# An AdaLN and grouped-expert FFN kernel: expert tiles in another order, rounded terms first, and one weight store and one load of scales moved

## What is computed

```
h      = einsum('bct,bcd->bdt', x, weights[conditions])        # 4096 tokens x 256
scores = sigmoid(h @ gate_w.T)
sb     = scores + gate_bias
# group score: sum of the 2 largest of 8; the 2 best of 4 groups; in them the 8 largest sb
wsel   = scores[chosen 8]; wsel = wsel / wsel.sum() * 2.5       # cw: zero elsewhere
x_lat  = h @ fc1_w.T                                            # 128 wide
y_lat  = sum over experts e of cw[:, e] * relu2(x_lat @ w1[e].T) @ w2[e].T
shared = relu2(h @ shared_up_w.T) @ shared_down_w.T             # 512 wide inside
out    = x + shared + y_lat @ fc2_w.T                           # relu2(v) = relu(v) ** 2
```

## Time and profile before

| | |
|---|---|
| median of 3 runs | 429.77 us (428.74 to 430.76) |
| profiled execution, its own time | 426.48 us |
| its span | 424.7 us |
| PE, DVE, ACT, POOL busy | 91%, 72%, 61%, 50% |
| span from the projection's first product to the first expert product | 15.4 to about 163 us |
| large expert tiles, then the three small ones | to about 383 us, then to 407 us |
| last product on PE; last add issued; end | 407.6; 416.7; 424.7 us |

### The profile page before, as it was taken

One profiled execution on the slowest core, in us unless ns is written; L12 is line 12 of the kernel. 1 busy time (PEld: TensorE's weight loads), 2 busy tenths in 40 slices (PEclk: granted clock), 3 DMA queues, 4 the chain that ended last, 5 costly groups with the idle time before them and its releaser, 6 DMA issues.

```text
span 424.7 us, 7288 instructions
## 1 busy us (share of the span) xinstructions
PE 387.3 (91%) x2261; PEld 337.1 (79%) x2261; DVE 303.8 (72%) x607; ACT 259.0 (61%) x351; POOL 213.2 (50%) x189
## 2 busy tenths in 40 slices
PE   8799999999999979889999999999999999999920
PEld 8789889998898977678888888888877888889920
DVE  0168697698947655698888888888887888887600
ACT  2176163735556454487778787787877778777710
POOL 5000567677767442006544675654644356385561
PEclk9899999999999998999999999999999999999975
DMA  5992494923857369889999999989999999998542
GB/s 160 261 316 69 108 366 141 319 67 114 271 186 224 65 184 342 249 264 249 306 280 300 263 277 227 230 209 315 331 347 267 216 211 255 352 329 181 84 49 25
DMA packets 67467, 95.67 MB, mean 225 GB/s; under 512 B 19999, under 2 KB 48790, under 8 KB 66838
## 3 DMA queue, kind: packets, MB, share of 16 engines
q1 hardware_dynamic: 52786, 79.81, 58.1%
q0 software_dynamic: 13936, 15.09, 20.7%
q10 hardware_dynamic: 708, 0.32, 0.3%
HBM read 94.48 MB, written 30.18 MB: 294 GB/s over the span
## 4 chain that ended last, share of the span: by engine, by line
PE 66%; DMA 8%; DVE 7%; issue 6%; ACT 5%; POOL 4%; SPq 2%; POOLq 1%; DVEq 0%; ACTq 0%
PE h_banks L763 19%; PE y_banks L784 18%; PE y_banks L712 9%; PE h_banks L694 6%; PE t_banks L802 5%; PE t_banks L649 4%; POOL out_x L594 3%; PE h_banks L627 3%; DVE act_lo L1103 2%; DMA out_x<-res,sid_sb 2%; DMA w_ring<-w_dram 2%; DMA cond_bd<-s_dram 2%; PE t_banks L722 1%; ACT scaled L915 1%; PE t_banks L667 1%
## 5 line engine op out<-in xcount | busy, mean ns | idle before, releaser
L594 POOL DMA_INDIRECT out_x<-res,sid_sb x70 | 123.8, 1769 | 91.5 <-ACT res L987 52.6
L1103 DVE TENSOR_TENSOR act_lo<-act_full,act_hi 128x1024 fp32r<-128x1024 f32 (+3 forms) x92 | 105.7, 1149 | 21.8 <-ACT act_full L943 11.5
L1379 DVE SCALAR_TENSOR_TENSOR scaled<-h_banks,cond_bd 128x1024 f32<-128x1024 f32 (+3 forms) x76 | 86.4, 1137 | 27.9 <-PE h_banks L763 27.7
L553 POOL DMA_INDIRECT rows_dram<-payload,slot_idx x64 | 68.7, 1074 | 43.6 <-DVE payload L1221 18.5
L763 PE MATMUL h_banks<-xc_hi,w_ring 128*128 128x512 f32 (+1 forms) x272 | 86.7, 401 | 3.5 <-issue 1.5
L941 ACT ACTIVATE act_hi<-scaled 128x1024 fp32r<-128x1024 f32 (+3 forms) x76 | 75.0, 986 | 4.5 <-DVE scaled L1379 4.2
L943 ACT ACTIVATE act_full<-scaled 128x1024 f32<-128x1024 f32 (+3 forms) x76 | 74.7, 983 | 0.0
L784 PE MATMUL y_banks<-act_hi,w_ring 128*128 128x512 f32 (+1 forms) x272 | 71.3, 384 | 0.4 <-ACT act_hi L941 0.4
L784 PEld LDWEIGHTS y_banks<-act_hi,w_ring 128*128 128x128 f32 x272 | 50.2, 188 | 10.8 <-ACT act_hi L941 0.5
L763 PEld LDWEIGHTS h_banks<-xc_hi,w_ring 128*128 128x128 f32 x272 | 46.0, 189 | 15.0 <-issue 5.7
L763 PE MATMUL h_banks<-xc_lo,w_ring 128*128 128x512 f32 (+1 forms) x136 | 52.4, 385 | 0.0
(11 more groups left out here) (191 smaller groups left out, 692.3 us busy)
## 6 DMA issues: line engine op xcount, KB each, us to landing
w_ring<-w_dram SPq DMA_DIRECT2D x68, 512.0 KB
cond_bd<-s_dram SPq DMA_DIRECT2D x64, 512.0 KB, 6.1
w_dram<-w_ring SPq DMA_DIRECT2D x8, 1024.0 KB, 7.8
x_in<-in_x SPq DMA_DIRECT2D x8, 512.0 KB, 6.2
res<-in_experts_raw SPq DMA_DIRECT2D x4, 1024.0 KB
out_x<-x_in SPq DMA_DIRECT2D x8, 512.0 KB, 3.8
rows_sb<-rows_dram SPq DMA_DIRECT2D x16, 256.0 KB, 5.5
rows_dram<-in_pad_rows SPq DMA_DIRECT2D x5, 328.0 KB, 4.4
```

Source lines behind the costliest of these rows:

```text
L553: pool.indirect_dma_start(rows_dram, bass.IndirectOffsetOnAxis(ap=slot_idx[:, which, n:n + 1], axis=0), payload[:, n, :], None).then_inc(r ...
L594: pool.indirect_dma_start(out, bass.IndirectOffsetOnAxis(ap=sid_sb[:, i % SID_RING, j, GROUP_SIZE:PER_GROUP], axis=0), res[:, i % 2, j * H ...
L1103: dve.tensor_tensor(lo, full, hi.bitcast(f32), ALU.subtract).then_inc(act_lo_ready, 1)
L1379: dve.scalar_tensor_tensor(pair(scaled, i, u), h, 0.0, scale, ALU.max, ALU.mult).then_inc(scaled_ready, 1)
```

## The change

It has four parts; all products, their sizes and their number stay the same.

1. `ORDER` gives the sequence of tiles: large tiles 0 to 13, the 384-row tile, large tile 14, the 256-row tile, large tile 15, the 128-row tile. A tile's *position* is its place in that sequence; `PLACE` gives it. Weight slots, table entries and semaphores follow the tile's number, buffers that alternate follow its position. The weights of tiles 14, 15 and of the last small tile are asked for when their slot's previous user is done (`next_weights`).
2. In `gate_and_latent`, `shared_up`, `shared_down` and `experts_up` all matmuls on the rounded (`hi`) part of the activations come first, for all output blocks; the wait for the remainder (`lo`) stands only before the last third.
3. The fourth split's stores are issued by POOL, right behind its last scatter; SP waits for them before tile 1's weights (`splits_stored(1)`).
4. Tile 1's scales are asked for as soon as their buffers are free: unit 0's before the wait for the split and tile 1's weights, unit 1's right behind these, units 2 and 3 before the loop over tiles.

```diff
-ROWS_OF = [BT] * BIG_TILES + [BT * (GROUPS - 1 - n) // GROUPS for n in range(SMALL_TILES)]
+ORDER = [*range(BIG_TILES - 2), BIG_TILES, BIG_TILES - 2, BIG_TILES + 1, BIG_TILES - 1, BIG_TILES + 2]
+PLACE = {t: i for i, t in enumerate(ORDER)}
+ROWS_OF = [BT if t < BIG_TILES else BT * (GROUPS - 1 - t + BIG_TILES) // GROUPS for t in ORDER]
...
         def user_before(i):
-            return BIG_TILES - 2 if i == X_TILES - 1 else i - 2
+            return PLACE[BIG_TILES - 2 if ORDER[i] == X_TILES - 1 else ORDER[i] - 2]
...
             def splits_stored(slot):
                 for w in range(2):
-                    sp.wait_ge(w_stored[slot][w], GROUPS // 2 * DMA)
+                    sp.wait_ge(w_stored[slot][w], (GROUPS // 2 - slot) * DMA)
+                if slot == 1:
+                    sp.wait_ge(last_split_stored, 2 * DMA)
...
-            store_split(3)
             store_shared(6)
             read_group(1)
+            load_scale(1, 0)
             splits_stored(1)
             for u in range(PAIRS):
                 load_weights(1, u)
+            load_scale(1, 1)
             load_rows(2)
             store_shared(7)
+            for u in range(2, PAIRS):
+                load_scale(1, u)
+            next_weights = {user_before(i) + 1: i for i in range(2, X_TILES)
+                            if ORDER[i] < BIG_TILES or ORDER[i] == X_TILES - 1}
...
             for k in range(BATCHES):
                 scatter(k)
+            for w in range(2):
+                pool.wait_ge(w_hi, 2 * (GROUPS - 1) + w + 1)
+                pool.wait_ge(w_lo, 2 * (GROUPS - 1) + w + 1)
+                pool.dma_start(w_dram[SPLIT_ORDER[GROUPS - 1], :, :, w], w_ring[:, (GROUPS - 1) % 2, :, w].bitcast(f32))\
+                    .then_inc(last_split_stored, DMA)
...
             def shared_down(u):
                 b, slot = divmod(u, 2)
                 pe.wait_ge(act_hi_ready, u + 1)
-                pe.wait_ge(act_lo_ready, u + 1)
...
+                for v, parts in ((act_hi, (small_hi, small_lo)), (act_lo, (small_hi,))):
+                    if v is act_lo:
+                        pe.wait_ge(act_lo_ready, u + 1)
+                    for j in range(BT):
+                        for m in range(2):
+                            k = 2 * slot + m
+                            for w in parts:
+                                first = v is act_hi and m == 0 and w is small_hi
+                                last = pe.matmul(
...
             def experts_up(i, u):
                 if u == 0:
                     pe.wait_ge(x_hi_ready, i + 1)
-                    pe.wait_ge(x_lo_ready, i + 1)
...
+                for n in range(3):
+                    if n == 2 and u == 0:
+                        pe.wait_ge(x_lo_ready, i + 1)
+                    for m in range(2):
+                        w = w_slot(i, u)[:, 0, 1 if n == 1 else 0, m * P:(m + 1) * P]
+                        v = (x_lo if n == 2 else x_hi)[:, i % 2, 0:SIZE[i]]
```

More of the change, by code:

```diff
@@ L568, in _ @@
             for i in range(X_TILES):
[L569 removed]
+                row = pool.value_load(table[0:1, T_ROW + ORDER[i]:T_ROW + ORDER[i] + 1], min_val=0, max_val=DUMMY)
                 src = rows_dram[bass.ds(row, SIZE[i]), LAT:LAT + PER_GROUP].bitcast(i32)
@@ L643, in gate_and_latent @@
                         pe.wait_ge(rank_read, ranks[0])
-                for j in range(BT):
-                    terms = [t for a in range(HALVES) for t in three(
-                        *(v[:, b % XC_RING, a, j * P:(j + 1) * P] for v in (xc_hi, xc_lo)),
-                        *(w[:, GF0 + a * GF:GF0 + (a + 1) * GF] for w in (small_hi, small_lo)))]
-                    for n, (v, w) in enumerate(terms):
-                        last = pe.matmul(gf_tiles[:, j // 2, j % 2, :], v, w, start=n == 0, stop=n == len(terms) - 1)
+                for v, parts in ((xc_hi, (small_hi, small_lo)), (xc_lo, (small_hi,))):
+                    if v is xc_lo:
+                        pe.wait_ge(xc_lo_ready, b + 1)
+                    for j in range(BT):
+                        for a in range(HALVES):
+                            for w in parts:
+                                first = v is xc_hi and a == 0 and w is small_hi
+                                last = pe.matmul(
+                                    gf_tiles[:, j // 2, j % 2, :], v[:, b % XC_RING, a, j * P:(j + 1) * P],
+                                    w[:, GF0 + a * GF:GF0 + (a + 1) * GF],
+                                    start=j % 2 == 0 and first, stop=j % 2 == 1 and v is xc_lo and a == HALVES - 1)
                 last.then_inc(lat_ready, 1)
@@ L685, in shared_up @@
                 pe.wait_ge(xc_hi_ready, b + 1)
[L686 removed]
                 s = take_slot("u", u)
[L688 to L695 removed]
+                for v, parts in ((xc_hi, (small_hi, small_lo)), (xc_lo, (small_hi,))):
+                    if v is xc_lo:
+                        pe.wait_ge(xc_lo_ready, b + 1)
+                    for m in range(2):
+                        k = 2 * (u % 2) + m
+                        for a in range(HALVES):
+                            for w in parts:
+                                first = v is xc_hi and a == 0 and w is small_hi
+                                last = pe.matmul(
+                                    h_banks[:, s, m * BANK:(m + 1) * BANK],
+                                    w[:, UP0 + a * SHARED + k * P:UP0 + a * SHARED + (k + 1) * P],
+                                    v[:, b % XC_RING, a, :], start=first, stop=v is xc_lo and a == HALVES - 1)
                 last.then_inc(up_ready, 1)
```

86 lines of the change are left out of this document (35 added, 51 removed).

## The result

| | before | after |
|---|---|---|
| median | 429.25 us (426.47 to 430.76, 4 runs) | 413.22 us (407.94 to 415.28, 4 runs) |
| ratio | 1 | 0.9556 [0.9441, 0.9672] |

The medians are 16.0 us apart, a ratio of 0.963; the ratio above counts only the faster two of after's four runs, since the other two fell into a slower state. The changed kernel was run three more times as a yardstick for the experiments: 0.9664 [0.9613, 0.9716], 0.9631 [0.9579, 0.9683] and 0.9630 [0.9580, 0.9680], a gain of 14 to 16 us. The rows of after come from the profiled execution of the third of these (412.37 us of its own time, span 410.3), since the very first profiled one was the slowest of its four. It is 14.1 us under the profiled execution before (426.48).

What follows compares the result with a forecast made beforehand. PE, busy 91% of 424.7 us, was taken as the bound, with time to win only at its idle places and tail. 2.0 + 2.9 + 3.7 − 0.5 = 8.1 us off gave 421.7 us, range 416.5 to 426.5.

Steps and rivals of the forecast that it cites:

- 0.9 goes: Tile 1's first up product: of PE's 1.04 us wait at 174.24 for the remainder of x, 0.9 us goes.
- Rounded terms in the shared stage: Last `shared_down`: 16 of 24 products run ahead of the act_lo wait, filling 1.9 us and avoiding 1.7 us of slow clock.
- The split from GpSimd: Last split's two 1 MB stores move from SP to GpSimd: raw scales land 2.5 us later, leaving the stage 2.0 us gain.
- The second tile's scales: Step from tile 0 to tile 1: scales loaded 6 us sooner remove PE's 1.97 us wait; with 0.9, 2.9 us gained.
- Small tiles among the large: Tail after the last y rounding: no adds wait for overlapping tiles after position 13, 18.35 us becomes 14.7, gain 3.7 us.
- The charge for late scales: Large tile after a 256-row tile gets its scales late: 0.5 us charged, ends 0 and 2.
- The first: Rival at the raw scales: their small pieces slip between the split's large ones, gain grows by 2.5, 419.2 us; chance 0.2.
- the third: Rival: PE waits 2 to 4 us for scales or weights at large tiles between small ones, about 424.7 us; chance 0.1.
- The second: Rival at the tail: it does not shrink, GpSimd being held by something other than overlap, 425.4 us; chance 0.12.
- the fourth: Rival, slower: raw scales stand behind the whole split, 432.2 us at 13 us of delay; chance 0.04.

## Why the prediction was wrong

**The step that failed** is the reading of the bound: "from there to the last large tile PE runs almost without a gap". The gaps are there, one per tile, 0.11 us each, and the six matmuls behind each take 0.22 us longer. Both edits on this wait, alone in the kernel before and undone in the new one, move the pace between 13.33 and 12.98 us, which is 4.9 and 3.9 us of time. The forecast had the mechanism in hand: it charged the same wait at 174.24 with "0.9 goes", once, and rightly (with the up order alone the first two tiles take 32.6 us instead of 33.5). But it went by rows of PE with idle time in brackets, and this row has none. The hint stood elsewhere in the trace: eight waits of the weight loads between 190 and 300 us, and identical groups of six, 1.39 us everywhere but 1.61 once per tile. With 3.5 us for it the sum would have been 11.6, a time of about 418, inside the range; the measured 413.22 is another 5 us below that. In the profile the tail and the last stretch make 2.2 of these and the first two stages 0.6; the rest is that the forecast kept 3.3 us between profile and median, and only 0.9 were left (413.22 − 412.37).

**Rounded terms in the shared stage**: right in mechanism and size. Undone, the 2.2 us of idle time and the fall of the clock come back as described. From unit 15's relu to the first expert product it takes 5.8 us in all 13 profiles with the new waits there, and 9.3, 9.0 and 10.1 in the three with the old ones. The whole stage gives 2.4 us in this profile (2.0 forecast), but 0.6 to 5.2 over the four profiles of the kernel, so the close agreement of the sum is in part luck.

**The split from GpSimd**: the charge was fair, but the worth of the move was missed. GpSimd's cost is 0.8 us a store, not up to 3.8 (the forecast charged neither). The Trainium skill, "DMA: Bandwidth & Descriptors", section "Anatomy of one DMA — SWDGE (gpsimd) path", calls the generation of descriptors by GpSimd small, and the 0.81 and 0.75 us agree. The delay of the raw scales, charged at 2.5, is real: from their issue to unit 15's relu it takes 9.0 to 9.95 us in three kernels where they meet no split, 11.2 to 11.8 in six profiles where they do, 14.1 to 14.3 in three more. But the forecast saw the move only as a cost: undone together with the scales' it costs 7.0 us, because tile 1's weights then wait for a split that lands 10.4 us (median) after its issue on SP, and PE's clock falls behind the wait.

**The second tile's scales**: the size of the stage is right (3.1 us, forecast 2.9), but it isn't these loads that bring it: at their old place the time is the same. The forecast argued as if SP kept its old times, and gave to the scales what the split's move brings; that the size fits is luck.

**Small tiles among the large**: the sign and the place are right, and both sizes low. The tail shrinks by 4.8 us, not 3.7: the first add of position 17 went out 2.1 us before the last y rounding, not 1.4, and the third found its result ready, so the last add came 5.5 us after that rounding, not 6.7; the 8.0 us from there to the end are as said. The charge for late scales was 0.5 us, measured 0.6 to 1.7.

**The rivals.** The first (the split doesn't hold the raw scales) was wrong in its cause; its 419.2 us is nearer to the measured time than the forecast only by chance. Of the third, a trace remains in the last stretch. The second and the fourth did not come. The sum was not undone by one of them: of the 6.3 us by which this profile beats the forecast, 3.5 are the pace, 2.2 the last two stages, and 0.6 the first two.

## What to carry to other kernels

Hold the durations of identical groups of matmuls against each other, and read the waits of the weight loads beside those of the matmuls, before calling a steady stage dense: a group that is a sixth longer once per tile was a wait here, and it counts as often as there are tiles. Where two edits shorten the same chain, undo each alone and both together; here one carries all of it and also protects what a third edit gained upstream. A transfer that delays something is worth removing only if the next thing on the same engine isn't as late.

## What was not expected of the hardware

A wait of 0.11 us on PE cost 0.33 us in all: the six matmuls behind it took 1.61 us against 1.39 without a break, at a granted clock of 1.00 (220 to 240 us) in both kernels. The same 1 MB store landed after a median of 10.8 us when SP issued it at 156 us, behind tile 0's scales, after 6.2 us when GpSimd issued it at 143 us, and after 7.1 when GpSimd issued it at 152 us, beside tile 0's scales; why it is so much slower from SP is not shown. And the raw scales, asked for 0.7 to 1.0 us after GpSimd began its first store in each case, reached the first root seed after 4.8 to 5.4 us in six profiles and after 7.7 to 7.9 in three.
